# Moving three loads and a few matmuls of a cross-attention kernel: query packs first in each unit, two x chunks one unit later, GpSimd behind the turned sums

## The reference, cut to what matters

```python
q = heads(x @ to_q_w)                                   # x: 16 batches x 512 tokens x 640 channels
for keys, (to_k, to_v) in four groups of the context:   # 77 text, 4 object, 4 other tokens, the rest (427)
    s = q @ heads(keys @ to_k).T / sqrt(32)
    out += softmax(s) @ heads(keys @ to_v)              # a softmax of its own for each group
y = merge(out) @ to_out_w + to_out_b + x
```

## Time and profile before

| | before |
|---|---|
| median of 3 runs | 2438.07 us (2430.52 to 2440.12) |
| profiled execution | 2437.21 us, its span 2435.6 us |
| granted TensorE clock, mean | 0.994 |
| PE busy | 2389.4 us, 98% |
| DVE busy | 1845.9 us, 76% |
| ACT busy | 1778.7 us, 73% |
| POOL busy | 412.3 us, 17% |
| DMA | 370.10 MB, 152 GB/s mean |

### The profile page before, as it was taken

One profiled execution on the slowest core, in us unless ns is written; L12 is line 12 of the kernel. 1 busy time (PEld: TensorE's weight loads), 2 busy tenths in 40 slices (PEclk: granted clock), 3 DMA queues, 4 the chain that ended last, 5 costly groups with the idle time before them and its releaser, 6 DMA issues.

```text
span 2435.6 us, 37404 instructions
## 1 busy us (share of the span) xinstructions
PE 2389.4 (98%) x12801; PEld 1806.8 (74%) x12801; DVE 1845.9 (76%) x3288; ACT 1778.7 (73%) x3909; POOL 412.3 (17%) x567
## 2 busy tenths in 40 slices
PE   7999999999999998999999999999999999999998
PEld 7899999998999984566666666666666666666654
DVE  3356777732333478999999999999999999999992
ACT  3243433322222359999999999999999999999994
POOL 0000000000000023423133133122133132222210
PEclk9999999999999999999999999999999999999999
DMA  9545444374644657677677677677687677677751
GB/s 283 145 144 165 152 141 141 124 255 144 231 160 175 202 134 148 133 142 146 132 150 156 128 147 153 136 151 148 132 156 147 130 151 155 132 148 140 146 127 50
DMA packets 346820, 370.10 MB, mean 152 GB/s; under 512 B 94334, under 2 KB 241918, under 8 KB 346630
## 3 DMA queue, kind: packets, MB, share of 16 engines
q1 hardware_dynamic: 293232, 304.79, 56.0%
q10 hardware_dynamic: 53398, 62.93, 7.5%
HBM read 215.57 MB, written 83.89 MB: 123 GB/s over the span
## 4 chain that ended last, share of the span: by engine, by line
PE 87%; DVE 6%; ACT 4%; issue 1%; ACTq 1%; DMA 1%; SPq 0%
PE st_ps L1499 16%; PE s_ps L440 11%; PE om_ps L492 11%; PE st_ps L460 11%; PE om_ps L474 11%; PE om_ps L515 8%; PE s_ps L1551 7%; PE om_ps L1551 4%; PE s_ps L1519 3%; PE st_ps L1551 3%; DVE negmax L668 2%; ACT s_ps L608 2%; ACT probs L600 1%; ACTq L1222 1%; DMA qpack<-q_out 1%
## 5 line engine op out<-in xcount | busy, mean ns | idle before, releaser
L608 ACT ACTIVATE s_ps<-s_ps,negmax 128x427 f32<-128x427 f32 x1280 | 768.8, 609 | 23.3 <-DVE small L677 23.2
L668 DVE TENSOR_REDUCE negmax<-s_ps 128x2 f32<-128x854 f32 x640 | 666.2, 1041 | 81.8 <-PE s_ps L440 74.0
L600 ACT ACTIVATE probs<-st_ps 128x1024 f32<-128x1024 f32 x632 | 656.8, 1039 | 28.0 <-PE st_ps L460 13.0
L1499 PE MATMUL st_ps<-ctx_split,w_split 128*128 128x428 f32 (+2 forms) x2280 | 432.5, 350 | 11.2 <-DVE k_out L1379 10.8
L1499 PEld LDWEIGHTS st_ps<-ctx_split,w_split 128*128 128x128 f32 x2280 | 413.2, 191 | 29.2 <-DVE k_out L1379 11.9
L440 PE MATMUL s_ps<-kpack,qpack 96*128 96x512 f32 x1280 | 423.6, 412 | 10.8 <-ACT s_ps L608 7.5
L460 PE MATMUL st_ps<-qpack,kpack 104*128 104x512 f32 x1264 | 408.6, 404 | 8.7 <-ACT probs L600 8.5
L400 POOL TENSOR_TENSOR small<-small,negmax 128x616 f32<-128x616 f32 x160 | 196.4, 1227 | 1084.1 <-DVE negmax L685 1084.0
L440 PEld LDWEIGHTS s_ps<-kpack,qpack 96*128 96x128 f32 x1280 | 221.8, 189 | 194.3 <-ACT s_ps L608 91.1
L492 PE MATMUL om_ps<-xs,wq 128*128 128x512 f32 x1200 | 342.2, 395 | 5.0 <-DVE out L748 4.1
L515 PE MATMUL om_ps<-heads,wo 128*128 128x512 f32 x1125 | 322.8, 394 | 0.0
(11 more groups left out here) (103 smaller groups left out, 2318.4 us busy)
## 6 DMA issues: line engine op xcount, KB each, us to landing
kpack<-kT SPq DMA_DIRECT2D x240, 256.0 KB, 4.2
qpack<-q_out SPq DMA_DIRECT2D x240, 256.0 KB, 7.6
kT<-k_out ACTq DMA_DIRECT2D x160, 217.5 KB, 3.3
ctx_split_raw<-in_ctxT SPq DMA_DIRECT2D x128, 214.0 KB, 4.6
tok_pair<-in_ctxT SPq DMA_DIRECT2D x48, 512.0 KB, 4.4
xs_raw<-in_xT SPq DMA_DIRECT2D x85, 256.0 KB, 5.3
out<-in_xT SPq DMA_DIRECT2D x75, 256.0 KB, 5.6
out_yT<-out SPq DMA_DIRECT2D x75, 256.0 KB, 2.2
```

The lines of the kernel that those rows point to most:

```text
L600: nc.scalar.activation(probs[:, at:at + 2, :], transposed(u, duo), ACT.Exp).then_inc(p_done, 1)
L608: last = nc.scalar.activation(s_ps[:, n % 2, z, SMALL:TOK], s_ps[:, n % 2, z, SMALL:TOK], ACT.Exp, bias=negmax[:, r, IP, j, t:t + 1], accu ...
L668: nc.vector.tensor_reduce(negmax[:, r, IP, j, t0:t0 + 2], s_ps[:, n % 2, :, SMALL:TOK], AX_X, ALU.max, negate=True).then_inc(s_max, 1)
L1499: last = nc.tensor.matmul(k_place(run, m)[:, 0:n], w[name][:, pw, q, m * P:(m + 1) * P], c[b][:, px, q, a:a + n], start=(q == 0 and z == 0 ...
```

## The change

The query pack leads SyncE's order in each unit, and `load_residual` follows it. The x chunks 3 and 4 move from the end of unit w (w % 5 = 0) to unit w + 1, between the query pack and the residual. GpSimd waits for `lse_turned` of the same unit before it splits chunks 3 and 4. In units 0, 2, 3 and 4 the query products move from steps 2 to 6 to steps 1, 2, 3 and 5. Nothing is added to or taken from the arithmetic or the transfers.

```diff
-Q_AHEAD_FIRST = {2: (0, 3), 3: (3, 7), 5: (8, 11), 6: (11, 15)}
-Q_BEHIND_FIRST = {4: (7, 8)}
+Q_AHEAD_FIRST = {1: (0, 4), 2: (4, 8), 3: (8, 12), 5: (12, 15)}
+Q_BEHIND_FIRST = {}
...
         def slot(w):                                  # SyncE
-            if unit(w - Y_SLOT) and w - Y_SLOT < LAST:
-                load_residual(w - Y_SLOT)
             if w == UNITS - FIRST:
                 load_last_residuals()
             if w > 0 and unit(w + 3):
                 pack_queries(w + 3)
+            if w % QC == 1 and unit(w + 4):
+                load_x(w + 4, range(X_EARLY, QC))
+            if unit(w - Y_SLOT) and w - Y_SLOT < LAST:
+                load_residual(w - Y_SLOT)
             if w > 0 and unit(w + 1):
                 load_values(w + 1)
...
             if unit(w + 4):
                 pack_keys(w + 4)
-            if w % QC == 0 and unit(w + 5):
-                load_x(w + 5, range(X_EARLY, QC))
...
             if x_due:                                 # GpSimd
+                pool.wait_ge(lse_turned, w + 2)
                 for c in range(3, QC):
                     split_x(m, c)
```

## The result

| | before | after |
|---|---|---|
| median | 2434.44 us of 4 runs (2430.52 to 2440.12) | 2465.55 us of 4 runs (2462.99 to 2469.19) |
| ratio, 95% interval | | 1.0129 (1.0114 to 1.0144) |
| profiled execution | 2437.21 us, span 2435.6 | 2466.39 us, span 2464.8 |
| granted clock, mean | 0.994 | 0.987 |

The change makes the kernel 1.3% slower. The forecast was 2456 us, range 2438 to 2474, with 0.63 on slower by over 0.5%.

The account below looks back on a forecast made before the run. TensorE, busy for 98% of the span, was taken as the bound, so any new wait costs its full length. The terms -10.5 + 26.7 + 1.0 + 1.4 + 0 = +18.6 on 2437.2 us gave 2456 us, range 2438 to 2474.

Parts of the forecast that it names:

- The holds go (-10.5): Fourteen units splitting x: GpSimd's wait ends the holds of VectorE's small operations, L748 starts earlier; at most 10.5 us gained.
- The price of the wait: Splits and less_max behind GpSimd's wait end later, yet before they are needed, by 1 us or more; put at 0.
- Residuals of the fourteen at 13.3 us, 26.7 us lost: Fourteen units with x chunks: residual lands 13.3 us in, L748 waits, 1.91 us lost per unit, 26.7 us in all.
- last of the same bytes lands when the last did: SyncE's queue, fourteen units: the residual, now last, lands about when the pack did as last, 13.48 us (upper end).
- Landing in the order of issue: SyncE's one queue: all these transfers land in the order in which they are issued.
- Plain units, 1.0 us: Plain units: residual lands like the old pack, 10.9 us mean against 11.4 needed; 1 us lost in total.
- Unit 76, 1.4 us: Unit 76: residual behind five last residuals and the pack lands up to 4.5 us later; 0 to 4 lost, 1.4 taken.
- The first units, 0: Units 0, 2, 3, 4: paced by ScalarE, moved queries fill TensorE's idle time; 0, with 1 us either way.
- Rival D: TensorE's granted clock falls in first units and behind waits: +6, 2462 us; counted within the forecast's 0.55 chance.
- part 2: SyncE's queue: the new order of pack, chunks 3 and 4, residual makes L748 wait, up to 3 us each.
- Rival B: Fourteen units: residuals land by 11.4 us even behind pack and chunks; 2427 us, -0.4%; chance 0.10.
- C: All units: residuals late, since a load's tail behind a pack is 0.6 us longer; +45, 2482 us; chance 0.13.

Follow-up runs that it names:

- e2: Kernel before with only GpSimd's wait for the turned sums added: 2432.62 us, ratio 0.998 to the kernel before.
- e4: Changed kernel with load_residual back at the head of each unit and the first units' queries as before: 2432.04 us, 0.9983 to the kernel before.
- e1: Kernel before with only the first units' query products moved to steps 1, 2, 3 and 5: 2441.7 us, ratio 1.002.
- e6: Kernel before with the first units' query products three to a step in steps 1, 2, 3, 5 and 6: 2435.19 us, ratio 0.9992.
- e7: Kernel before with the first units' query products three to a step in steps 2, 3, 5, 6 and 7: 2434.09 us, ratio 0.9999.
- e10: Kernel before with GpSimd's wait, unit 76's last residuals behind the values, and each residual issued one unit earlier: 2444.1 us, ratio 1.0031.
- e3: Kernel before with only SyncE's new order, without GpSimd's wait and with the first units as before: 2468.65 us, ratio 1.0108.

## Why the prediction was right, and where its sizes were off

The direction, the mechanism, its place and the range were right. By its steps:

- **The holds go (-10.5).** Right, somewhat too large. e2 shows 7 to 8 us of it in the profile and 0.2% in the time (interval 0.1% to 0.3%). The price of the wait was put at 0, and it is: the splits end at 15.4 us in e2 and by 17.4 in the kernel after, and no wait of TensorE for x appears in either. That L748 loses nothing to a split beside it was read from its 0.71 us in two units, but in the kernel before no GpSimd operation ran beside any L748, so those rows could not show it. The kernel after does: 0.75 us beside a split and 0.75 us in 23 units without one, so the 1.1 us a unit that the sentence feared did not come.
- **Residuals of the fourteen at 13.3 us, 26.7 us lost.** The mechanism is right, e4 proves it. The landing was 12.77 us in the mean of the kernel after; L749's starts past 11.47 add up to 19.9 us against 26.7, and clock falls in units 41 and 71, which the sum had at nothing, bring the excess to 23.7. The fourteen were not alike: in units 21, 26 and 66 the residual landed by 11.6 us and cost next to nothing, in units 11 and 71 it cost over 3 us. So the net of the two steps was forecast as +16.2 and measured as +13.2 (over all profiles: 25.4 with order and wait, 11.5 with the old order and no wait, +13.9). That the two come so near is partly luck: the landing was put 0.5 us too late, worth 7 us over fourteen units, and the falls of the clock gave over half of that back. The equality "last of the same bytes lands when the last did" was 0.7 us too late (13.48 against 12.77). A likely reason, not tested alone: in the kernel before, each pack DMA lands 1.7 to 1.8 us behind the one ahead of it in the median, and in plain units of the kernel after a residual lands 0.7 us behind the pack, so the end of the old order was the slow pack's.
- **Landing in the order of issue.** Nearly right. In unit 11 of the kernel before, the residual, issued ahead of the pack, landed 12.03 us in, behind the first two pack DMAs (10.02 and 11.71). The sum does not hang on it.
- **Plain units, 1.0 us.** Mis-sized. In 15 plain units of the kernel after a residual kept L749 past 11.5 us, in unit 8 with a landing 12.1 us in, and these units cost 6.5 us. The mean landing was 0.2 us later than forecast (11.1 against 10.9), and the spread was known: the packs whose times stood in for the residuals had a standard deviation of 0.60 us, with 8 of 56 later than 11.4, and the residuals had 0.58. By the prediction's own working those times cost 1.7 us as they are, and 4.2 us if 0.19 us later. So the reason that it gave for 1 us, a margin of 0.5 us as more than the usual spread, is the step that failed. Five profiles with the residual last give 5.0 to 9.1, against 0.1 to 0.8 without.
- **Unit 76, 1.4 us.** Over all profiles units 76 to 79 take 71.4 us with the residual behind the pack and 69.8 in those without, so the size of the difference, 1.6 us, is right; the 3.6 us between the first two profiles is mostly a quick end of the one before.
- **The first units, 0.** This step failed most plainly. It said that ScalarE paces them and TensorE's idle time hides the move; the term didn't ask what TensorE is left with in steps 6 and 7. Rival D did, with the mechanism and +6; measured +4.5 (e1, e6, e7), and 6.3 between the two profiles. D's other half, falls behind the waits of part 2, came true in units 41 and 71.

The sum was forecast as +18.6 and is 29.3 in the profiles and 31 in the medians. From the means over the profiles: 4.5 + 13.9 + 6.0 (plain units, 6.5 with order and wait against 0.5 in the old order) + 1.6 = 26 us. The rest, 3 to 5 us, differs from run to run (the part before unit 0 alone starts the attention anywhere from 909 to 919 us) and isn't settled. Rival B fell with every profile of the new order; C, late residuals in every unit, happened in 15 of 57. The time stayed in the range because the range left room for D and a part of C; the sum alone was 11 to 12 us short.

## What to carry to other kernels

In a queue that is full, putting one transfer first means putting another last: find the transfer that has the least to spare when it comes last, and give it the head, whatever its size. Here the last transfer of a plain unit lands at about 11 us; the residual is needed by 11.4, the pack by 13.9 (in e2 and e10 TensorE waited for packs that landed later than that). A margin of half a microsecond on a mean landing is no margin when single landings come up to 1.2 us behind the mean. A wait that keeps GpSimd off VectorE's short SBUF operations is worth its price when, as here, what it delays has microseconds to spare.

## What the runs showed of the hardware

A fall of the granted clock follows a wait too. In nine of the profiles, with late residuals or packs, 20 units from 6 to 75 had 1.5 to 3.6 us of idle PE and a mean clock of 0.86 to 0.93. Eighteen of them lost 1.7 to 2.1 us more than their idle time, and two lost 3 us more (unit 31 of e3, 3.23 us idle and 24.85 us long, and unit 51 of e10, 2.55 us idle and 24.30 us long). Nineteen units of all the profiles with as much idle time kept the clock at 1.00, among them unit 11 after with 3.29 us. What decides between the two isn't shown.

In the kernel after, a 256 KB load from DRAM that follows a pack in the queue landed 0.7 us behind it in the median of the plain units, 0.5 us at the least and 1.8 at the most. In the kernel before, the same load ahead of the pack landed 5.1 to 7.0 us into every plain unit, median 5.6.
